# A four-layer graph network: whole products in the edge network, fades, lane scores and compared numbers in PSUM

## What is computed

```python
# layer 0, an edge network
edge_in  = concat([h[src], h[dst], edge_attr_64])
hid      = relu(edge_in @ We1 + be1)              # 32 wide
edge_msg = relu(hid @ We2 + be2)                  # 128 wide
h2       = relu(concat([h[dst], edge_msg]) @ Wn1 + bn1)   # 64 wide
node_msg = relu(h2 @ Wn2 + bn2)                   # 128 wide
x        = x + h + segment_sum(node_msg, dst)
# layer 1, attention with 4 heads
e   = elu(s_src[src] + s_tgt[dst], 0.2)
ex  = exp(e - segment_max(e, dst)[dst])
x   = x + segment_sum(ex / segment_sum(ex, dst)[dst] * xp[src], dst)
# layer 2, attention with 8 heads, leaky relu, no maximum taken off
# layer 3, relations
x = x + h @ w_self.T + scatter_add(h[dst] @ W[edge_type], src)
```

## Time and profile before

| | us |
|---|---|
| median of three runs | 4735.3 |
| lowest, highest | 4725.31, 4736.79 |
| the profiled execution | 4749.68 |
| span of its instructions | 4747.9 |

### The profile page before, as it was taken

The page is one execution under the profiler, slowest core; times in us unless marked ns, Lnnn a source line. Parts: engine busy times, 40 slices in busy tenths (PEclk is TensorE's granted clock), DMA queues, the critical chain, the costliest instruction groups (busy, mean ns, idle before and its releaser), DMA issues. The chain is left out here.

```text
span 4747.9 us, 82711 instructions
## 1 busy us (share of the span) xinstructions
PE 3500.8 (74%) x18822; PEld 2815.3 (59%) x18822; DVE 2650.5 (56%) x8500; ACT 1355.3 (29%) x4722; POOL 3336.3 (70%) x3373
## 2 busy tenths in 40 slices
PE   4999999999488888888758988889977433334333
PEld 2555555555477777777748877778863333333333
DVE  6677667665356566666665666666555333333332
ACT  4444444443344444444432222222222000000000
POOL 4777777776577777777527777777741777777776
PEclk8999999999555555555565555555558555555555
DMA  4555454441343333433312223332225222222222
GB/s 94 111 105 99 88 88 88 88 91 28 106 99 100 100 101 100 97 100 98 68 39 60 74 72 77 81 86 60 55 72 195 53 51 51 51 51 52 51 51 57
DMA packets 489982, 378.46 MB, mean 80 GB/s; under 512 B 307216, under 2 KB 442170, under 8 KB 486443
## 3 DMA queue, kind: packets, MB, share of 16 engines
q0 software_dynamic: 106496, 184.24, 17.5%
q1 hardware_dynamic: 383272, 192.14, 16.9%
HBM read 327.50 MB, written 33.83 MB: 76 GB/s over the span
## 5 line engine op out<-in xcount | busy, mean ns | idle before, releaser
L1193 POOL DMA_INDIRECT gat_row<-tab,gat_index x832 | 850.0, 1022 | 296.3 <-issue 222.0
L1193 POOL DMA_INDIRECT mlp_row<-tab,mlp_index x832 | 841.6, 1012 | 308.1 <-issue 241.0
L1193 POOL DMA_INDIRECT rel_row<-tab,rel_index x832 | 817.5, 983 | 283.7 <-issue 236.9
L1193 POOL DMA_INDIRECT att_row<-tab,att_index x832 | 802.3, 964 | 265.1 <-issue 250.0
L1564 PE MATMUL rel_ps_sum<-rel_row,rel_hot 128*128 128x128 f32 x1664 | 426.0, 438 | 658.5 <-DMA rel_row<-tab,rel_index 636.3
L1564 PEld LDWEIGHTS rel_ps_sum<-rel_row,rel_hot 128*128 128x128 f32 x1664 | 370.5, 328 | 714.6 <-DVE rel_hot L1587 396.3
L1791 PE MATMUL gat_ps_sum<-gat_row,gat_hot 128*128 128x136 f32 x1664 | 441.6, 446 | 179.4 <-ACT gat_sums L1740 128.9
L1986 PE MATMUL att_ps_sum<-att_row,att_hot 128*128 128x136 f32 x1664 | 443.1, 446 | 121.2 <-DVE acc L1496 116.9
L1791 PEld LDWEIGHTS gat_ps_sum<-gat_row,gat_hot 128*128 128x128 f32 x1664 | 387.6, 330 | 194.4 <-ACT gat_hot L1734 123.1
L1496 DVE TENSOR_TENSOR acc<-acc,rel_ps_sum 128x128 f32 x416 | 119.6, 287 | 678.6 <-PE rel_ps_sum L1564 648.7
L1986 PEld LDWEIGHTS att_ps_sum<-att_row,att_hot 128*128 128x128 f32 x1664 | 379.2, 324 | 196.9 <-DVE acc L1496 192.4
(11 more groups left out here) (275 smaller groups left out, 6092.6 us busy)
## 6 DMA issues: line engine op xcount, KB each, us to landing
mlp_aim<-in_dst SPq DMA_DIRECT2D x416, 128.0 KB
gat_aim<-in_dst SPq DMA_DIRECT2D x416, 128.0 KB
mlp_row<-in_edge_attr SPq DMA_DIRECT2D x416, 64.0 KB
tab<-n_stage SPq DMA_DIRECT2D x25, 1024.0 KB
mlp_row<-tab,mlp_index POOLq DMA_INDIRECT x832
gat_row<-tab,gat_index POOLq DMA_INDIRECT x832
att_row<-tab,att_index POOLq DMA_INDIRECT x832
rel_row<-tab,rel_index POOLq DMA_INDIRECT x832
```

Of the source, the lines that this page charges most:

```text
L1193: gp.indirect_dma_start(rows[n][b][:, t, :], None, tables[n], bass.IndirectOffsetOnAxis(index[b][:, n, t:t + 1], axis=0)).then_inc(s_g[b], 16)
```

## The change

**`edge_mlp`.** The target's terms of both hidden layers are one product of 96 columns per half: `mm_dst` writes partitions 0 to 63 (for `h2`) and 64 to 95 (for `h1`) of one bank `p_h`, all 512 edges wide. The other hidden products lose their two halves beside each other: `mm_h1`, `mm_em` and `mm_h2` are one product of 512 edges, and `mm_nm` has its four tiles of 128 edges all on rows 0 to 63. `p_h` and `p_sum` become two banks each. ACT's and DVE's work on them is 512 wide with the same number of instructions. `hot` compares with a copy of `iota` in PSUM.

```diff
-            def mm_q(k, q, b):
-                ge(pe, s_h2r, k)
+            def mm_dst(k, q, b):
+                ge(pe, s_h2r, k - 1)
...
-                for n, edges, to_h1, to_h2 in sides(b):
-                    mm = pe.matmul(to_h2, dst[b % RING][:, n, 0:HID2], hot_t[b % RING][:, edges],
-                                   start=True, stop=False)
+                for n in range(2):
+                    edges = slice(n * HALF, (n + 1) * HALF)
+                    mm = pe.matmul(p_h[b % 2][0:IN_D, edges], dst[b % RING][:, n, :], hot_t[b % RING][:, edges],
+                                   start=(n == 0), stop=False)
...
-                for n, edges, to_h1, to_h2 in sides(b):
-                    pe.matmul(to_h1, dst[b % RING][:, n, HID2:IN_D], hot_t[b % RING][:, edges], start=True, stop=False)
...
-                for n, edges, to_h1, to_h2 in sides(b):
-                    mm = pe.matmul(to_h1, g.we1_row[:], row_t[b % 2][:, edges], start=False, stop=True)
-                mm.then_inc(s_h1, 1)
+                pe.matmul(p_h[b % 2][HID2:IN_D, :], g.we1_row[:], row_t[b % 2][:], start=False, stop=True
+                          ).then_inc(s_h1, 1)
...
-                for n in range(2):
-                    rows = slice(n * HID2, n * HID2 + HID1)
-                    mm = pe.matmul(p_em[:, n, :], g.we2[rows, :], h1[b % 2][rows, :],
-                                   start=True, stop=True)
-                mm.then_inc(s_em, 1)
+                pe.matmul(p_em[:], g.we2[HID2:IN_D, :], h1[b % 2][HID2:IN_D, :], start=True, stop=True).then_inc(s_em, 1)
...
-                for n, edges, to_h1, to_h2 in sides(b):
-                    mm = pe.matmul(to_h2, g.wn1_msg[:], em[b % 2][:, edges], start=False, stop=True)
-                mm.then_inc(s_h2, 1)
+                pe.matmul(p_h[b % 2][0:HID2, :], g.wn1_msg[:], em[b % 2][:], start=False, stop=True).then_inc(s_h2, 1)
...
-                for t in range(2):
-                    for n in range(2):
-                        rows = slice(n * HID2, (n + 1) * HID2)
-                        mm = pe.matmul(p_nm[:, n, t * P:(t + 1) * P], h2[b % 2][rows, t * P:(t + 1) * P],
-                                       g.wn2[rows, :], start=True, stop=True)
+                for t in range(TILES):
+                    mm = pe.matmul(p_nm[:, t * P:(t + 1) * P], h2[b % 2][:, t * P:(t + 1) * P], g.wn2[0:HID2, :],
+                                   start=True, stop=True)
...
-            pipeline(pe, [(1, turn), (3, mm_h2), (2, mm_h1), (4, mm_sum), (2, mm_em), (3, mm_nm), (2, mm_q)])
+            pipeline(pe, [(1, turn), (3, mm_h2), (2, mm_dst), (2, mm_h1), (4, mm_sum), (2, mm_em), (3, mm_nm)])
```

```diff
-                for bank, to in ((p_loc, lane_loc), (p_e, lane_e)):
-                    ins = act.copy(in_lane(to), bank[0:LANES, :].rearrange("l (h t p) -> l h t p", h=2, p=P))
-                ins.then_inc(s_laned, 1)
+                act.copy(lane_loc, p_loc[0:LANES, :]).then_inc(s_laned, 1)
...
-            pipeline(act, [(0, lay), (0, bring_tgt), (4, at_end(bring_local)), (5, at_end(fifth_exp)),
-                           (6, at_end(to_lanes)), (9, at_end(weight)), (14, measure_gap), (15, make_hot), (19, keep_sum), (21, at_end(fade_exp))], WIDE)
+            pipeline(act, [(0, lay), (4, bring_tgt), (23, keep_sum), (18, measure_gap), (19, make_hot),
+                           (8, at_end(bring_local)), (9, at_end(fifth_exp)), (10, at_end(to_lanes)), (13, at_end(weight)),
+                           (25, at_end(fade_exp))], WIDE)
...
-                v.tensor_tensor_scan(lane_run, same[:, 0:BLOCK], lane_e, 0.0, ALU.mult, ALU.max).then_inc(s_run, 1)
+                v.tensor_tensor_scan(lane_run, same[:, 0:BLOCK], p_e[0:LANES, :], 0.0, ALU.mult, ALU.max).then_inc(s_run, 1)
...
                 v.wait_ge(s_fade, n + 1)
+                v.tensor_copy(fade[:, side(b)], faded[:, side(b)]).then_inc(s_shown, 1)
+                v.wait_ge(s_shown, n + 1)
...
-                    v.tensor_tensor(split, split, fade[:, side(b), 0, i].unsqueeze(2).broadcast_to([P, H, f + 1]),
+                    v.tensor_tensor(kept.rearrange("p (h f) -> p h f", h=H), split,
+                                    fade[:, side(b), 0, i].unsqueeze(2).broadcast_to([P, H, f + 1]),
                                     ALU.mult).then_inc(s_mul, 1)
                     v.wait_ge(s_mul, n + 1)
-                    v.tensor_tensor(there, there, sums[:, side(b), i, 0:W].unsqueeze(1), ALU.add).then_inc(s_acc, 1)
+                    v.tensor_tensor(there, kept.unsqueeze(1), sums[:, side(b), i, 0:W].unsqueeze(1), ALU.add).then_inc(s_acc, 1)
```

```diff
-                v.tensor_tensor(hot[b][:], g.iota[:].unsqueeze(1).broadcast_to([P, TILES, P]),
+                v.tensor_tensor(hot[b][:], iota.unsqueeze(1).broadcast_to([P, TILES, P]),
```

More of the change, by code:

```diff
@@ L1217, in edge_mlp @@
         own = [c.sb(f"own{b}", [P, TILES]) for b in range(2)]
-        p_row, p_h1, p_h2, p_sum = (c.ps(n) for n in "row h1 h2 sum".split())
-        p_em, p_nm = (c.ps(n, (P, 2 * BLOCK))[:].rearrange("p (h f) -> p h f", h=2)[:, :, 0:HALF]
-                      for n in ("em", "nm"))
+        p_row, p_em, p_nm, p_iota = (c.ps(n) for n in "row em nm iota".split())
+        p_h, p_sum = ([c.ps(f"{n}{b}") for b in range(2)] for n in ("h", "sum"))
+        iota = p_iota[:, 0:P]
         s_g, s_tick = c.sems("g", UNROLL), c.sem("tick")
@@ L1338, in turn @@
                 mm.then_inc(s_turn, 1)
-            def sides(b):
-                edges = (slice(0, HALF), slice(HALF, BLOCK))
-                return [(n, edges[n], p_h1[n * HID2:n * HID2 + HID1, 0:HALF],
-                         p_h2[n * HID2:(n + 1) * HID2, 0:HALF]) for n in range(2)]
-            def mm_q(k, q, b):
-                ge(pe, s_h2r, k)
+            def mm_dst(k, q, b):
+                ge(pe, s_h2r, k - 1)
                 pe.wait_ge(s_hot_t, k + 1)
@@ L1411, in _ @@
             ch = Chain(v, s_neg)
-            v.memset(p_h1[:], 0.0)
+            ch.do(v.tensor_copy(iota, g.iota[:]))
             for b in range(2):
@@ L1532, in relation_sum @@
         row = [c.sb(f"row{b}", [P, TILES, D]) for b in range(UNROLL)]
-        p_sum = [c.ps(f"sum{b}") for b in range(2)]
+        p_sum, p_iota = [c.ps(f"sum{b}") for b in range(2)], c.ps("iota")
+        iota = p_iota[:, 0:P]
         s_g, s_word, s_tick = c.sems("g", UNROLL), c.sems("word", UNROLL), c.sem("tick")
-        s_ix, s_hot, s_sum, s_acc, s_node, s_turn, s_loc = (
-            c.sem(n) for n in "ix hot sum acc node turn loc".split())
+        s_ix, s_hot, s_sum, s_acc, s_node, s_turn, s_loc, s_iota = (
+            c.sem(n) for n in "ix hot sum acc node turn loc iota".split())
         block = c.block()
@@ L1570, in _ @@
         def _(v):
+            v.tensor_copy(iota, g.iota[:]).then_inc(s_iota, 1)
+            v.wait_ge(s_iota, 1)
             def decode(k, q, b):
@@ L1615, in softmax_sum @@
         lane = g.TMP[0:LANES].rearrange("p a f -> p (a f)")
-        lane_loc, lane_e, lane_run, lane_top, lane_mark = (lane[:, n * BLOCK:(n + 1) * BLOCK] for n in range(5))
+        lane_loc, lane_run, lane_top, lane_mark = (lane[:, n * BLOCK:(n + 1) * BLOCK] for n in range(4))
         same = lane[:, 5 * BLOCK:6 * BLOCK + 1]
@@ L1865, in fades @@
                 v.wait_ge(s_most, 3 * n + 1)
-                old, new = fade[:, side(b), 0], fade[:, side(b), 1]
+                old, new = faded[:, side(b), 0], faded[:, side(b), 1]
                 v.tensor_tensor(old, most[:, 0:2 * GROUP, :], keep.unsqueeze(2).broadcast_to([P, 2 * GROUP, H]), ALU.mult)
```

52 lines of the change are left out of this document (24 added, 28 removed).

## The result

Over three executions of the changed kernel (4972.9 to 4973.93 us) the time is 1.0508 times the time before, 95% interval 1.0488 to 1.0529; the median of all four is 4973.58 us, against 4734.51 before. The fourth took 5985.68 us at a mean granted clock of 0.52 and is not in the ratio; it has no trace, so whether it was `edge_mlp` at the 1.2 GHz level, which is one of the rivals, is open. The profiled execution took 4972.9 us, its span is 4971.1 (before: 4747.9).

The account below looks back on a forecast made before the run. POOL's gathers were taken to bound the block loops, with PE also near its limit in `edge_mlp`. Terms +317 (`edge_mlp`), -66 (`softmax_sum`) and -30 (`relation_sum`) gave +221 on the median 4735.3: 4956 us, range 4878 to 5025.

Parts of the forecast that it names:

- The step of PE: In `edge_mlp`, PE's time per block goes from 5.07 to 6.77 us and sets the loop: +312 us, +317 with +5.
- cheap small products: Rival, `edge_mlp`: small products are cheap in themselves, not by lying beside each other; total 4594 us; chance 0.05.
- The overlap of neighbours: Rival, `edge_mlp`: `mm_em` and `mm_nm` run together, step 5.8 us, total 4754; chance 0.05.
- The clock: Rival, `edge_mlp`: PE is granted 1.2 GHz, step about 12.3 us, total near 6200; chance 0.02.
- The kept chain: Rival, `softmax_sum`: another wait replaces `keep_sum`, -20 us instead of -66, total 5002; chance 0.15.
- -71 for -66: `softmax_sum` term: earlier `keep_sum` and fewer held gathers bring a group to 40.8 us, -66 us; bounds -35 to -80.
- Both idle times of PE: `softmax_sum`, once a group: PE's waits of 3.32 us for `keep_sum` and 3.64 before the sum shrink; chain 39.2 to 35.2.
- the sign that no gather waits over 0.5 us: Sign, `softmax_sum`: no gather waits over 0.5 us once a group, with a mean near 965 ns.
- -31.9 for -30: `relation_sum` term: gathers held 36 ns each, 832 of them, are freed, -30 us; bounds 0 and -30.
- who would be named for the waits in `edge_mlp`: Sign, `edge_mlp`: gathers wait for PE's `turn`, some 1.7 us a block.
- The upper bound of 5045: Whole kernel: `edge_mlp` step of 6.95 us with the least gains, 4735 + 360 - 35 - 15 = 5045 us.
- its own lower bound of 4881: Whole kernel: `edge_mlp` step of 6.5 us with larger gains, 4735 + 256 - 80 - 30 = 4881 us.

Follow-up runs that it names:

- e5: The changed kernel with `mm_nm` as a pair again and `iota` back in SBUF: 5893.42 us, ratio 0.9932 to the kernel before, in runs where every kernel took longer.
- e4: The kernel before with only the changed `softmax_sum` operands in PSUM, ACT's list in the old order: 4717.7 us, ratio 0.9971.
- e3: The kernel before with only ACT's list in `softmax_sum` in the new order: 4701.35 us, ratio 0.9937.
- e2: The kernel before with the changed `softmax_sum` and `relation_sum`, `edge_mlp` left as before: 4646.43 us, ratio 0.9818.
- e1: The kernel before with only the changed `edge_mlp` products, its `iota` in SBUF: 5061.15 us, ratio 1.0695.

## Why the prediction was right, and where it was off

**The step of PE** decided it. The forecast took the widths of the pairs apart, 0.43 us of streaming and 0.02 to 0.22 around it, and put 0.86 in place of 0.43 in five parts: 6.77 us. Measured is 6.81, part by part in the rows above (forecast in brackets): `turn` 0.57 (0.54), `h2` 1.00 (1.02), `dst` 1.04 (1.02), `h1` 0.97 (0.97), `sum` 1.09 (1.08), `em` 1.05 (1.06), `nm` 1.09 (1.08). Two small misses nearly cancel in the loop, which is luck: the step is 0.04 longer (8 us), and 16.6 us, not 5, lie behind the last gather, because POOL is further ahead of PE at the end (the last `turn` ends 15.7 us behind the last gather, 3.6 before). Loop and gap together are +325.8 for +317.

**Of the rivals**, cheap small products (4594) fell by this step, and e5 shows why: `nm`'s own records cost 0.65 us beside each other and 1.09 alone. The overlap of neighbours (4754) fell by the 0.52 us between the starts of `em`'s last record and `nm`. The clock was 0.99 in the profiled execution, so that rival fell there. Its own terms, with a step of 12.3 us, add up to about 6105 rather than 6200. The kept chain (5002) fell by 0.54 us of waiting where 1.41 had been. Its idea, that one wait can swallow what another edit saves, does show in e4: what the gathers save goes into a longer wait, and only the new order in the same change prevents it.

**`softmax_sum`**: -71 for -66. Both idle times of PE went as worked out, yet the chain ends at 36.16 us, not 35.2, and the sign that no gather waits over 0.5 us did not come true (0.54). The missing microsecond lies ahead of the part that the forecast looked at. It took as given how long the group's rows need behind the last gather until `add_terms` can start: 1.96 us at the median before, 2.08 in e3 and 2.04 in e4, but 3.12 after and 3.27 in e2, where both edits are in and the gathers follow each other more closely. Why the rows come later there was not found. It costs little, since POOL alone would be only 0.24 us sooner: the period is 40.88 us for the forecast's 40.8, with 0.1 less held than allowed and 0.24 more for the chain, which is partly luck. What is still held is 15.4 us a loop or 0.6 a group, where 0.7 had been left, and most of it lies beside the second scan.

**`relation_sum`**: -31.9 for -30, against the profiled execution. Here the forecast was right on the wrong footing. It carried a sum that was read from the profiled execution over to the median unchanged. The change's own profiled forecast, 4971, met 4972.9; the median came out at 4973.6, not 14 under it. The profiled execution of before had more held gathers than other traces of that code have, and the edit takes away what is held, so it also takes away that surplus. The term for the median should have been nearer 16 us. This is nearly all of the 17.6 us between 4956 and 4973.6, and the same 14 us that e2 was short of. That `relation_sum` is where the surplus lies rests on e1, e3 and e4, which run its old code in 1053 to 1061 us; a second trace of the kernel before is not there to show it.

**Missed altogether**: who would be named for the waits in `edge_mlp`. The size was right, 1.7 us a block (measured 339 / 208 = 1.63), the place not: not PE's `turn`, but ACT's copy of the indices, behind `em_relu`. The time is the same, since ACT follows PE. It would matter to someone who tried to help this loop by another buffer for the rows.

**Slips that changed nothing.** The step of the cheap small products adds up from its own terms to 5.05 us, not 4.9; the total of 4594 stays. The upper bound of 5045 uses 360 where the step's bound had been 355, and the range begins at 4878, just under its own lower bound of 4881.

## What to carry to other kernels

Before merging small products into one, look in the trace at whether they ran beside each other in the array: compare a pair's time with the streaming of its columns one after the other; if it is half, five products fewer can cost a third more. Where a chain on one engine and another engine's own pace are close, time the edits together, since each alone is capped by the other (28 and 16 us alone, 71 together). A chain starts where its data lands, so look at that wait again after the change. And when an edit removes a loss that varies from run to run, take its worth from the median run, not from the one that was profiled.
